# Causal linear attention with its scores and A.v in 64-token chunks instead of 128, in a fused macaron block on one core

## What is computed

```python
def ffn(x):                       # x: (16, 1024, 512)
    s = einsum('btd,dm->btm', x, Win) + bin_               # M = 64
    h = relu(s[..., None] * W1 + b1)                       # 16 inner values for each m
    g = einsum('btmh,mh->btm', h, W2) + b2
    return einsum('btm,md->btd', g, Wout) + bout

def attn(x):                      # 16 heads of D = 32
    q, k, v = split(x @ w_attn, 3)
    q, k = elu(q) + 1, elu(k) + 1
    # for each token: S += k v^T; z += k; y = (q S) / (q.z + 1e-6)
    return linear_attention(q, k, v) @ w_proj

x = x + 0.5 * ffn(layernorm(x))   # called L1
x = x + attn(layernorm(x))        # L2
x = x + 0.5 * ffn(layernorm(x))   # L3
```

## Time and profile before

| | us |
|---|---|
| median of 3 runs | 2464.65 (2463.72 to 2464.97) |
| the profiled execution | 2462.28 |
| its span, first to last instruction | 2460.6 |

### The profile page before, as it was taken

How to read it: one execution, slowest core, us unless ns; L and a number is a source line. 1 busy time by engine, 2 the same in 40 slices (tenths; PEclk the granted TensorE clock), 3 DMA queues, 4 the chain that set the end, 5 groups by cost and what they waited for, 6 DMA issues and landing times.

```text
span 2460.6 us, 76187 instructions
## 1 busy us (share of the span) xinstructions
PE 2326.5 (95%) x33474; PEld 1796.0 (73%) x33474; DVE 1908.5 (78%) x3346; ACT 1433.4 (58%) x2267; POOL 813.7 (33%) x869
## 2 busy tenths in 40 slices
PE   1699999999999999999999999999999999999995
PEld 1577777777777777777777777777777777777774
DVE  4577777888777788777788877778887778887756
ACT  3455655665655565665566565556566556656544
POOL 4323233323333323323332332333332333233222
PEclk8799999999999999999999999999999999999997
DMA  5000111110111110011111001111101111100000
GB/s 167 1 2 2 36 36 36 36 36 3 36 36 36 36 36 23 17 36 36 36 36 36 19 19 36 36 36 36 36 2 36 36 36 36 36 19 2 19 18 36
DMA packets 39356, 77.00 MB, mean 31 GB/s; under 512 B 4081, under 2 KB 4081, under 8 KB 39026
## 3 DMA queue, kind: packets, MB, share of 16 engines
q1 hardware_dynamic: 39026, 72.12, 8.6%
HBM read 38.56 MB, written 33.55 MB: 29 GB/s over the span
## 4 chain that ended last, share of the span: by engine, by line
PE 51%; DVE 23%; issue 15%; POOL 7%; ACT 3%; SPq 1%; DVEq 0%; DMA 0%; POOLq 0%
PE bank L967 20%; PE att L967 11%; DVE acc_psum L684 6%; PE att L1072 5%; POOL z L344 5%; DVE st L650 4%; PE att L1097 4%; DVE qT L738 3%; PE att L987 3%; DVE res L696 2%; DVE A L746 2%; PE att L1003 2%; DVE yl L666 2%; PE att L1042 1%; PE bank L1012 1%
## 5 line engine op out<-in xcount | busy, mean ns | idle before, releaser
L449 ACT ACTIVATE ffr<-ffs,b1c,w1c 128x512 f32<-128x512 f32 (+1 forms) x544 | 431.7, 813 | 38.8 <-DVE acc_psum L684 29.5
L336 POOL TENSOR_TENSOR res<-res,hbout 128x512 f32<-128x512 f32 x256 | 327.8, 1292 | 330.6 <-ACT xhat L434 330.5
L684 DVE SCALAR_TENSOR_TENSOR acc_psum<-ffr,w2c,acc_psum 128x512 f32<-128x512 f32 (+1 forms) x510 | 382.3, 750 | 34.5 <-ACT ffr L449 15.4
L348 POOL TENSOR_SCALAR_AFFINE_SELECT A<-A 128x512 f32<-128x512 f32 x256 | 156.5, 635 | 763.1 <-ACT A L411 763.1
L434 ACT ACTIVATE xhat<-res,nmr,rstd 128x512 f32<-128x512 f32 x384 | 303.6, 808 | 166.2 <-DVE xf L674 130.6
L650 DVE BATCH_NORM_STATS2 st<-res 128x6 f32<-128x512 f32 x384 | 261.7, 682 | 16.4 <-DMA res<-in_L_attn_x_dram 8.4
L674 DVE STREAM_TRANSPOSE xf<-xhat 128x512 f32<-128x512 f32 x256 | 174.8, 693 | 100.4 <-ACT xhat L434 100.4
L344 POOL TENSOR_TENSOR z<-qT,z 128x512 f32<-128x512 f32 x128 | 189.4, 1500 | 165.0 <-DVE zc L726 84.0
L411 ACT ACTIVATE A<-att 128x512 f32<-128x512 f32 x256 | 139.2, 596 | 143.4 <-PE att L1072 143.4
L967 PE MATMUL att<-xh,wa_h 128*128 128x512 f32 x524 | 207.2, 395 | 0.0
L967 PE MATMUL att<-xh,wa_l 128*128 128x512 f32 x524 | 207.2, 395 | 0.0
(11 more groups left out here) (126 smaller groups left out, 4988.4 us busy)
## 6 DMA issues: line engine op xcount, KB each, us to landing
res<-in_L_attn_x_dram SPq DMA_DIRECT2D x32, 1024.0 KB, 5.3
out_dram<-res SPq DMA_DIRECT2D x32, 1024.0 KB, 4.3
kT<-in_L_attn_w_attn_dram SPq DMA_DIRECT2D x1, 1024.0 KB, 5.1
qT<-in_L_attn_w_attn_dram SPq DMA_DIRECT2D x1, 1024.0 KB, 7.5
v<-in_L_attn_w_attn_dram SPq DMA_DIRECT2D x1, 1024.0 KB, 10.3
A<-in_L_attn_w_proj_dram SPq DMA_DIRECT2D x4, 256.0 KB, 11.7
win<-in_L_ffn_Win_dram SPq DMA_DIRECT2D x4, 128.0 KB, 6.0
z<-in_L_ffn_Wout_dram SPq DMA_DIRECT2D x2, 128.0 KB, 4.4
```

What stands on the lines that cost most here:

```text
L336: eng.tensor_tensor(r[:, t, :], r[:, t, :], hbout[:, :], ALU.add).then_inc(s_bias[half], 1)
L348: eng.affine_select(out=A[:, h, :, :], in_=A[:, h, :, :], compare_op=ALU.is_ge, fill=0.0, base=0, pattern=[[0, 4], [1, P]], channel_multip ...
L449: eng.activation(ffr[i % 2][p, :], ffs[p, :], ACT.Relu, bias=b1c[p, i:i + 1], scale=w1c[p, i:i + 1]).then_inc(s_hr, 1)
L684: eng.scalar_tensor_tensor(psum[p, :], r[p, :], w2c[p, i:i + 1], psum[p, :], ALU.mult, ALU.add).then_inc(s_hm, 1)
```

## The change

Everything in `scores`, `attend` and `update` goes by chunks of 64 tokens, c = 0 and 1 of a tile. For each head two score matmuls are issued (32 rows, 64 columns, 64 streamed), one for each chunk's own 64x64 square; their outputs stand at partitions 0 and 64, so that eight cells are in use. The square between the chunks (queries of chunk 1, keys of chunk 0) isn't computed any more; chunk 1 reads a state that already holds chunk 0. `update` makes two sums, of the first 64 rows and of all 128, in two runs of 16 matmuls; the state `S` becomes two buffers of two states each, `ktok` two buffers. `attend` takes q times S with 64 streamed, 32 matmuls for a tile, from the state before the tile for chunk 0 and from the one that holds chunk 0 for chunk 1, and A.v in row halves (64 rows by 32 columns, 64 streamed), again 32 matmuls. `place` puts the results of row groups 0 and 1 into one bank, at different partitions, and those of 2 and 3 into another. `key` and `update` are done for every tile now, the last of a sequence too.

`A` is half as large. The whole mask is two DVE multiplications a tile of 128x512; ACT's `score` and POOL's `mask` are gone. `st`, `mv`, `rstd` and `nmr` get a second buffer. In the lists, `key` and `update` come ahead of the scores they serve, `values` of tile 0 goes behind the projections, three of DVE's four `stats` (L1) and its first `update` go ahead of the attention, `channels` of tile 3 goes ahead of `ff_out`.

In the prologue SP loads block 1 second and `bout` third, and `w_proj` goes to the last block buffer; `ff_in` runs first for block 0, then for block 1; ACT normalises block 0 ahead of `hbout`, and splits two weight parts ahead of `ff_bias`; DVE takes block 1's sums into `ff_out` first and its L2 statistics behind block 0's `channels`; POOL moves the low part of `w_proj` behind `shift`.

Rows of the two programs follow; in the rows of the changed one, lines are those of the changed code. PE in the attention, before: L1061 is `key`, L1072 `scores`, L1108 `update`, L967 `outer`, L1088 and L1097 are q times S and A.v of `attend`, L1012 is `channels`.

```diff
+        A = sb("A", [P, 4, 4, HALF])
+        ktok = [sb(f"ktok{i}", [P, C]) for i in range(2)]
+
+        S = [sb(f"S{i}", [P, 2, 4, D]) for i in range(2)]
...
+        attended = att[:, :, :].rearrange("p (c j) (k n) -> p (j k) c n", c=2, k=2)[:, :, :, 0:HALF]
...
             load(0)
+            load(1)
+            eng.dma_start(z2[0:1, 1, :], bout.rearrange("(a n) -> a n", a=1)).then_inc(s_bout, 16)
             for h in range(4):
...
+            eng.dma_start(wa_st[1][:, :, :], wa_v[:, :, C:2 * C]).then_inc(s_wa[1], 16)
+            load(2)
+            for h in range(2):
+                eng.dma_start(z2[M * h:M * h + M, 0, :], Wout).then_inc(s_wo, 16)
+            for n in (0, 2):
...
+            wp_v = w_proj.rearrange("(k q1 j q0 e) n -> q0 q1 e j k n", k=2, q1=2, j=2, q0=2)
+            for q in range(4):
+                for j in range(2):
+                    eng.dma_start(wp_st[D * q:D * q + D, 2 * j:2 * j + 2, :], wp_v[q // 2, q % 2, :, j]).then_inc(s_wp, 16)
...
+            weights_lo(2)
             rstds(L2, 0)
-            weights_lo(2)
+
+            e.wait_ge(s_nmr[L2], 1)
+            weights_lo("p")
             rstds(L2, 1)
...
+                e.wait_ge(s_kt, nth(b, t))
+
+                e.wait_ge(s_up, nth(b, t) - 2)
+                copy(ktok[t % 2][:, :], bank[spot["key", b, t][0]][:, :], s_ktok)
...
+            def mask(b, t, pair):
+                h = slice(2 * pair, 2 * pair + 2)
+                e.wait_ge(s_tri, 4)
                 e.wait_ge(s_num, 4 * b + t)
-                e.wait_ge(s_walo, 4)
-                e.wait_ge(s_sc[h], 4 * b + t + 1)
-                eng.tensor_tensor(A[:, h, :, :], att[:, h, :].rearrange("p (g i) -> p g i", g=4),
...
+                src = bank[spot["up", b, t][0]][:, 0:2 * P].rearrange("p (c g n) -> p c g n", c=2, g=4)
+                e.wait_ge(s_up, n)
+
+                e.wait_ge(s_qS, n - 1)
...
+                    e.wait_ge(s_S, n - 1)
+                    eng.tensor_tensor(S[n % 2][:, :, :, :], src,
+                                      S[(n - 1) % 2][:, 0:1, :, :].to_broadcast([P, 2, 4, D]), ALU.add).then_inc(s_S, 1)
...
+            ff_out(1, 1, 0)
+            ff_out(1, 1, 1)
+            shift(L2, 0)
+            ff_out(1, 1, 2)
+            ff_out(1, 1, 3)
             for t in range(TILES):
                 channels(0, t)
+            for t in range(TILES):
+                stats_of_sum(L2, 1, t)
...
+                        for c in range(2):
+                            d = slice(D * h, D * h + D)
+                            w = slice(t * P + HALF * c, t * P + HALF * c + HALF)
+                            op = eng.matmul(att[HALF * c:HALF * c + HALF, h, g * HALF:(g + 1) * HALF],
+                                            kT[d, g, w], qT[d, g, w], start=True, stop=True)
+                op.then_inc(s_sc, 1)
...
+                carried_on = (False, True) if reads_none(b, t) else (True, True)
+
+                def place(c, g, h):
+                    quarter = 2 * (h % 2) + g % 2
+                    col = g // 2 * 2 * P
+                    return att[D * quarter:D * quarter + D, 2 * c + h // 2, col:col + HALF]
+
+                for c in range(2):
+                    w = slice(t * P + HALF * c, t * P + HALF * c + HALF)
+                    state = S[n % 2][:, 1, :, :] if c else S[(n - 1) % 2][:, 0, :, :]
+                    if carried_on[c]:
+                        for g in range(4):
+                            for h in range(4):
+                                d = slice(D * h, D * h + D)
+
+                                op = eng.matmul(place(c, g, h), state[d, g, :], qT[d, g, w],
+                                                start=g < 2, stop=False, skip_group_check=True)
+                op.then_inc(s_qS, 1)
+                e.wait_ge(s_v, n)
+                for g in range(0, 4, 2):
+                    for h in range(0, 4, 2):
+                        for c in range(2):
+                            k = slice(HALF * c, HALF * c + HALF)
+                            for g2 in (g, g + 1):
+                                for h2 in (h, h + 1):
+                                    op = eng.matmul(place(c, g2, h2), v[k, t, (4 * g2 + h2) * D:(4 * g2 + h2 + 1) * D],
+                                                    A[k, h2, g2, :], start=g < 2 and not carried_on[c], stop=True,
+                                                    skip_group_check=True)
+                op.then_inc(s_num, 1)
+
+            def update(b, t):
...
+                for c, k in ((1, HALF), (0, P)):
...
+                            op = eng.matmul(o[d, c * P + g * D:c * P + g * D + D], ktok[t % 2][0:k, n], v[0:k, t, n],
+                                            start=True, stop=True)
...
+            for n in range(2):
+                for part in range(PARTS):
+                    ff_in(-1, part, (n,))
...
                     ff_in(j, 1)
                 if on(j):
+                    update(j, 0)
                     den(j, 2)
                     den(j, 3)
                     values(j, 1, 1)
                     spread(j)
+                    key(j, 1)
+                    key(j, 2)
                     values(j, 2, 0)
+                    update(j, 1)
+                    scores(j, 0)
+                    key(j, 3)
                     values(j, 2, 1)
-                    scores(j, 0)
+                    attend(j, 0)
+                if on(j + 1):
+                    channels(j + 1, 0)
+                if on(j):
                     values(j, 3, 0)
-                    update(j, 0)
-                    attend(j, 0)
+                    scores(j, 1)
                     values(j, 3, 1)
-                if on(j + 1):
-                    channels(j + 1, 0)
...
```

542 lines of the change are left out of this document (232 added, 310 removed).

## The result

| | before | after |
|---|---|---|
| median, us | 2464.18 | 2570.33 (2563.66 to 2575.55, 4 runs) |
| ratio | | 1.043, 95% interval 1.0404 to 1.0455 |
| span of the profiled execution, us | 2460.6 | 2566.9 |
| start of the loop, us | 93.44 | 63.86 |
| from one round's `spread` to the next, mean of 31, us | 72.74 | 77.07 (74.4 to 80.1) |

The changed kernel is 4.3% slower; 2407 was forecast. The loop starts 29.6 us sooner and its rounds lose 4.3 us each, 134.4 between the first `spread` and the last, so the span grows by 106.3.

A forecast was written before the change was run, and what follows sets the result against it. The loop was taken as bound by the length of PE's list, the prologue by a walk through DVE, ACT and POOL. 2462.28 - 32.4 - 5 - 20 = 2404.9 profiled, median 2407 us; own range 2390 to 2420, 8 in 10 2388 to 2446.

The forecast's parts named there:

- prologue: Ahead of the loop: reordered work on DVE, ACT and POOL starts the loop at 61.0 us, -32.4 us.
- prices of groups, `key` with them: Loop: scores and A.v get cheaper, q times S, update and one more key dearer; -1.2 us per two rounds, -20 us.
- first rounds: Start of the loop: 4 us off the first round and 1 off the next two together, -5 us.
- What counts in this reading is the number of records on the fullest cell, not the number of records.: PE groups: price follows the fullest cell, 0.059 us per 64-column record plus 0.13 fixed for starting and draining.
- if a run of 64 or more small records is slower than one of 32: PE groups: a sign the prediction named in advance that would show it wrong.
- rival 2: PE groups: price per record, not per cell; at 12.2 ns loop +34, whole 2464; at 13.8 ns 2516; chance 0.10.
- which only a price per cell explains: Objection to rival 2: den's eight and sixteen records differ by 27 ns a record on four cells.
- I take waits as unchanged.: Loop: a possible stall of 0.2 us ahead of attend set against a covered 0.4 us wait of den; no change.
- step (c): Prologue: block 2's shift meets at most one POOL addition, so the first hidden step comes at 29.3, 20.4 us earlier.
- DVE as the bound: Attention: DVE replaces PE as the bound, each tile waits 0.15 to 0.3 us more; 2428 us taken, chance 0.19.
- rival 3: q times S: row groups sharing a bank through place take turns, +0.47 us a group, 56 us, 2463; chance 0.04.
- Rival 4: Prologue isn't shortened: a shift meets a weight part again or hidden steps slow down; 2430 us, chance 0.05.

The follow-up runs named there:

- e7: Changed kernel with both chunks' scores written to partitions 0 to 63, so the 64 records lie on four cells instead of eight; 2605.2 us, one run.
- e1: Kernel before with all of the changed kernel's prologue edits and its own old loop; 2431.7 us, ratio 0.9869 against before.
- e5: Changed kernel with three of a block's four update groups moved in PE's list, DVE's update moved likewise; 2644.3 us, ratio 1.0735 against before.
- e9: Kernel before with q times S in column halves, 64 records of 64 columns on all 16 cells, a bank per row group; 2490.9 us.
- e2: Kernel before with the matmuls of q times S issued twice, 64 records of 128 columns; 2514.6 us, ratio 1.0212 against before.
- e4: Kernel before with the matmuls of scores issued twice, 64 records of 128 columns on four cells; 2570.5 us, ratio 1.0439 against before.

## Why the prediction was wrong

**The sum.** What the loop and the prologue really did, against the profiled span:

| | forecast | measured |
|---|---|---|
| prologue | -32.4 | -29.6 |
| prices of groups, `key` with them | -20 | +43 |
| stops for instructions, 150 to 2330 us | 0 | +98 (104.2 - 6.2) |
| half clock behind stops, 150 to 2330 us | 0 | about +22 |
| `den` behind `zsum` | 0 | -7.6 (9.5 to 1.9) |
| first rounds | -5 | in the lines above (the first took 76.3, not 79.2) |
| together | -57 | +126; the span says +106.3 |

The second line is 8 x (0.843 - 1.11) + 8 x (0.789 - 1.02) + 7 x (0.785 - 0.44) + 0.38 + (8 x 0.776 - 7 x 0.39) + 0.4 = +2.7 for two rounds, times 16.

These lines come to 20 us too much, and the reason is in the second. Counted start by start from the first `spread` to the last, the rounds' 134.4 us are 110 of stops, 22 of half clock, and 2 for everything else. So by their medians the changed groups cost 43 more, but nearly all of it was won back in the loop, mostly by things that the second line doesn't price: `update` with the wait behind it had taken 0.53 on average and not 0.39 (15 us), and the groups of `key` and `channels` became shorter in the new order (0.52 to 0.40, 0.44 to 0.41; together 10 us less, although there is a `key` more a sequence), and `den`'s wait went. What made the kernel slower are the stops and the clock that fell behind them.

**First failed step: "What counts in this reading is the number of records on the fullest cell, not the number of records."** It was half of the rule. The forecast had named the sign of this itself ("if a run of 64 or more small records is slower than one of 32"), and it came: q times S went from 0.44 to 0.78. The slope between `den`'s 8 and 16 records is real, and e7 finds nearly the price per 64-column record that was interpolated (0.066 against 0.059). What was missing is the second bound: 64 records took no less than 0.78 in any run, however they lay. `scores` and A.v were forecast at 0.65 and 0.60 and came at 0.84 and 0.79, q times S at 0.65 and came at 0.78; `update` was right at 0.78, because its rows had been priced by what bounds them. In each group of the kernel before but `update` and q times S the cells were the slower of the two, so fits to those rows could not show the other. `update` and q times S did, at 12.2 and 13.8 ns a record; that was rival 2, given 0.10. Its objection, "which only a price per cell explains", told against feeding as the only bound, not against both. Rival 2's own number for 12.2 ns was +34 for the loop against the +43 measured. (Its whole times are 3 us too high for its own loops: they should have read 2461 and 2513.)

On the Trainium skill's floor of about 25 ns between matmuls ("TensorE: Matmul & The Clock Gate", "Wait — 56ns, not 53.3ns?") I wrote that the trace disagrees. That was a wrong unit: these matmuls have two records each, and `update` has 16 matmuls in 0.39, 24 ns each, q times S of the changed kernel 32 in 0.785, 24.5 ns. By the page, as an estimate, a group of 32 costs 0.80 and the loop's prices come to +44; so over a whole group the trace agrees, and I had argued the best warning away. Only inside a group does it not: the first 32 records (16 matmuls) start within 0.24 to 0.27 us, mostly 7 ns apart. In `scores`, q times S and A.v the next ones come after a pause of about 80 ns at 5 to 17 ns; in `update` both runs of 32 look alike, with a pause of 120 ns between them.

**Second failed step: "I take waits as unchanged."** I looked for waits on engines. The stops for instructions, 98 us, and the half clock behind them, about 22, are the largest part of the error, and neither the sum nor a rival had them. Rival 2 was nearly right in its prices and still 106 us short, mainly for this reason. The kernel before carries the sign but not the cost: 265 loads of 256 instructions, none closer than 3.3 us, half of them 6.75 us or more apart. With 395 loads half came within 3.98 us of the one before.

**The prologue was right**, in its steps and within 3 us in its sum. L1's normalising began at 11.33 (13 forecast), `ff_in` ran from 16.02 to 27.3 (17.5 to 27.5), from the first hidden step to L2's normalising it took 56.97 - 31.83 = 25.1 (25.1), and from there to the first projection 6.9 (6.6). The one miss is step (c), 31.83 instead of 29.3: `ff_bias` stands on ACT behind the weight copy for q, whose load only landed at 28.4. I had watched POOL there and not the loads. e1 shows that the step carries over to the total: 31.2 sooner, 31.5 less.

**The rivals.** DVE as the bound (0.19) did not come: PE's waits in the changed kernel name none on DVE's masks. e5 shows how near it is, since moving three groups brought 101 us of waits on DVE and POOL. The shared bank (rival 3) falls with e9, 0.785 with and without sharing; of the Trainium skill's restriction ("TensorEngine Tiling (Array Packing)", "Restrictions and Gotchas") no run here showed a cost. Rival 4 did not come either.

**What stays open:** why e2's second 32 records of 128 columns cost 0.57; why e9's rounds grew by 0.8 where the groups grew by 1.2, and e2's whole by 51 where its groups grew by 63; why only some of the long stops are followed by the half clock; and how many instructions PE holds ahead, since only the spacing of the loads and the places of the stops can be read.

## What to carry to other kernels

A group of small matmuls has two prices, its fullest cell and its number of records, and takes the larger: splitting matmuls to use more cells pays only until about 12 ns a record (24 ns a matmul). Before doubling the number of matmuls, count instructions (weight loads too) over the densest few us against loads of 256 that come no closer than 3.2 us, look at q8 on the page, and read the clock by stretches, since a stop can bring half speed behind it. And where PE's list leaves no gaps, each group in it covers someone's wait: moving one uncovers it.

## What the runs showed of the hardware

- PE's instructions come in loads of 16 KB, 256 instructions. The closest two in any run are 3.2 us apart; PE goes on 2.2 to 3.0 us after a load's start. In the changed kernel 100 of 159 gaps, and 104 of 129 us, stand at one and the same place in every 256 instructions.
- The first 32 records of 64 or fewer columns in a group start mostly 7 ns apart; in `scores`, q times S and A.v the next follow at 5 to 17 ns after a pause of 80 ns. 64 records take 0.785 in q times S, on 8 cells or on 16, and 0.84 in `scores`; 32 take 0.38 to 0.39.
- A 64-column record costs its cell 0.066 us and one of 128 columns 0.11 (e4: 0.89 for eight).
- 13 times in the changed kernel from 150 to 2330 us the granted clock was 0.50 (1.2 GHz), each time during or within 2 us after a stop of PE of 1.6 to 2.5 us: 47.8 us in all, at a cost of some 22. The kernel before had none there.
